# Gated cross-attention block: the first pass of head pair 0 is issued inside the last projection chunk, and the row-maximum matmul reads 2 rows

## The reference

```
x = x + tanh(g_xattn) * cross_attention(context, layernorm(x), mask)
x = x + tanh(g_ffn)   * ffn(layernorm(x))
cross_attention: k, v = split((context @ W_src.T + b_src) * mask);  q = (tgt @ W_tgt.T + b_tgt) * mask
                 8 heads of 64: softmax(q @ k.T / 8, keys with mask 0 at -inf) @ v, joined with tgt, @ W_out.T + b_out
ffn: 8-bit activations and ternary weights, 512 -> 2048, depthwise convolution of width 3, SiLU, 2048 -> 512
```

## Time and profile before

| | us |
|---|---|
| median of 3 runs | 1926.86 |
| the profiled execution | 1929.86 |
| its span, first to last instruction | 1928.0 |
| stages A and B up to the last matmul of chunk 7 | 610.69 |
| from there to the first score | 57.55 |
| first score to the end of the attention | 728 |

### The profile page before, as it was taken

How to read it: one execution, slowest core, us unless ns; L and a number is a source line. 1 busy time by engine, 2 the same in 40 slices (tenths; PEclk the granted TensorE clock), 3 DMA queues, 4 the chain that set the end, 5 groups by cost and what they waited for, 6 DMA issues and landing times.

```text
span 1928.0 us, 24398 instructions
## 1 busy us (share of the span) xinstructions
PE 1684.4 (87%) x8738; PEld 1038.8 (54%) x8738; DVE 1216.9 (63%) x2270; ACT 780.3 (40%) x793; POOL 729.0 (38%) x317
## 2 busy tenths in 40 slices
PE   6887899999997699999999999999856785967867
PEld 5666678888885344455445444544433443534434
DVE  6777645343433567755765676465269979799793
ACT  2111122222210044433442344245318766787676
POOL 1121000000000088866885688578606134062340
PEclk9989999999998599999999999999979798997988
DMA  6656547444444511114111412041130030120201
GB/s 233 229 181 206 179 170 243 154 149 152 171 145 152 180 56 56 56 66 143 56 57 66 143 57 100 12 143 35 44 131 1 1 131 0 38 92 0 88 1 44
DMA packets 104676, 200.59 MB, mean 104 GB/s; under 512 B 7568, under 2 KB 27024, under 8 KB 104592
## 3 DMA queue, kind: packets, MB, share of 16 engines
q1 hardware_dynamic: 104592, 199.49, 29.5%
HBM read 127.90 MB, written 71.57 MB: 103 GB/s over the span
## 4 chain that ended last, share of the span: by engine, by line
PE 62%; issue 19%; POOL 7%; DVE 6%; DMA 5%; SPq 1%; ACT 1%; POOLq 0%; DVEq 0%; ACTq 0%
PE ps L1260 13%; PE ps L1272 12%; PE ps L1224 9%; PE ps L1226 9%; PE ps L1225 9%; PE ps L1244 6%; DMA wraw<-in_w2T 5%; POOL h_first L672 4%; POOL h_third L672 2%; PE ps L1285 2%; DVE junk L926 1%; PE ps L1461 1%; DVE h_first L1179 1%; POOL acc L667 1%; DVE gp L1158 1%
## 5 line engine op out<-in xcount | busy, mean ns | idle before, releaser
L667 POOL TENSOR_TENSOR acc<-acc,pr 128x1024 f32<-128x1024 f32 x192 | 457.7, 2384 | 118.7 <-ACT pr L684 99.6
L684 ACT ACTIVATE pr<-ps,mcol 128x1024 f32<-128x1024 f32 x256 | 284.3, 1114 | 405.1 <-PE ps L1260 402.3
L926 DVE CUSTOM_DVE_ANT_0 junk<-ps,mbias 128x512 bf16<-128x512 f32 x512 | 333.4, 689 | 171.8 <-PE ps L1244 168.0
L1272 PE MATMUL ps<-pr,vv 128*64 128x512 f32 x1024 | 273.3, 616 | 0.0
L672 POOL TENSOR_TENSOR h_first<-h_first,last_tap 128x1024 f32<-128x1024 f32 x44 | 104.8, 2385 | 306.2 <-ACT last_tap L804 306.2
L650 POOL MEMSET nmt<- 128x128 f32 x1 | 0.2, 204 | 449.1 <-DMA w_ternary<-wtb 449.1
L1244 PE MATMUL ps<-kh,qh 64*128 64x512 f32 x512 | 136.8, 475 | 26.3 <-DVE nmv L926 17.6
L1244 PEld LDWEIGHTS ps<-kh,qh 64*128 64x128 f32 x512 | 57.5, 193 | 148.3 <-issue 101.7
L1419 PE MATMUL ps<-xiT,w1q 128*128 128x512 bf16 x512 | 125.1, 393 | 5.9 <-ACT xiT L790 5.9
L1461 PE MATMUL ps<-w2q,hq 128*128 128x512 bf16 x512 | 120.8, 390 | 2.5 <-ACT hq L840 1.8
L667 POOL TENSOR_TENSOR acc<-pr 128x1024 f32<-128x1024 f32 x32 | 76.8, 2399 | 110.8 <-ACT pr L684 110.8
(11 more groups left out here) (152 smaller groups left out, 3179.7 us busy)
## 6 DMA issues: line engine op xcount, KB each, us to landing
craw<-in_ctxT SPq DMA_DIRECT2D x8, 2048.0 KB, 9.7
xa<-in_x SPq DMA_DIRECT2D x8, 1024.0 KB, 6.4
wraw<-in_w1T SPq DMA_DIRECT2D x16, 512.0 KB, 7.3
wraw<-in_w2T SPq DMA_DIRECT2D x16, 512.0 KB, 7.6
q_split<-kqh SPq DMA_DIRECT2D x32, 256.0 KB, 2.0
q_split<-kql SPq DMA_DIRECT2D x32, 256.0 KB, 2.3
base<-lna SPq DMA_DIRECT2D x8, 1024.0 KB, 9.1
k_split<-kqh SPq DMA_DIRECT2D x32, 256.0 KB, 2.2
```

What stands on the lines that cost most here:

```text
L667: nc.gpsimd.tensor_tensor(acc[:, blk % 2, :], first, pr[:, (8 * blk + j) % NP, :], ALU.add).then_inc(pool_acc, 1)
L684: act.activation(pr[:, u % NP, :], ps[:, 2 * (u % 2):2 * (u % 2) + 2, :].rearrange("p a t -> p (a t)"), ACT.Exp, bias=mcol[:, (u // 64) * ...
L926: dve.tensor_tensor_reduce(out=junk[:, e, :], in0=ps[:, 4 + e, :], in1=mbias[:, b % 2, kk * CH:(kk + 1) * CH], scale=-1.0, scalar=3.0e38, ...
L1272: last = pe.matmul(ps[64 * e:64 * e + 64, 6 + blk % 2, :], vv[:, g % 2, j, 64 * e:64 * e + 64], pr[:, u % NP, e * CH:(e + 1) * CH], start= ...
```

## The change

The first 22 first-pass units are taken out of the front of stage C and put between the matmuls of chunk 7, on PE and on DVE. Up to unit 11 they use banks 4 to 7 in turn, from unit 12 to 21 banks 0 to 3, and a unit waits for the one two before it. `rows(0)` stands after the second value group. SP issues the loads of mask, `mcol`, `ql`, `kl` and `vv` before the stores of chunk 7, and stores and reads the row maxima between the stores of the values. ACT, not PE, now waits for the last stores of stage B, ahead of its first exponential.

```diff
@@ SP
             load_qk(0)
+            sp.wait_ge(pe_bv, (NCH - 1) * CT + 8)
+            load_mrow(0)
             load_qk(1)
+            sp.dma_start(mcol[:], mask_cols).then_inc(sp_mcol, 16)
+            load_lo(0)
...
+            load_vv(0)
             b_chunk(B - 1, 1, True)
@@ POOL
-            nc.gpsimd.memset(maug[:].bitcast(F32), 0.0).then_inc(pool_zero, 1)
@@ ACT, ahead of the first exp
+            act.wait_ge(dve_b, NCH * B_DVE_N)
...
+            act.wait_ge(sp_wq_out, 16 + 32 * NCH)
@@ order of the units
+        K_UNITS = {(m, part): 3 * m + part for m in range(PAIRS) for part in range(3)}
+        V_UNITS = {(0, 0): 12, (0, 1): 13, (0, 2): 14, (1, 0): 15, (2, 0): 16, (2, 1): 17, (2, 2): 18, (3, 0): 19, (3, 1): 20, (3, 2): 21}
@@ PE, unit n
+            if 2 <= n < LEAD:
+                pe.wait_ge(dve_free4, use4["t", 0] + 1 if n == 16 else use4["a", n - 2] + 1)
+                pe.wait_ge(dve_free5, use5["b", n - 2] + 1)
@@ PE, score
-                        last = pe.matmul(ps[:, 2 * (u % 2) + e, :], of_keys[64 * e:64 * e + 64, :], of_tokens[64 * e:64 * e + 64, :],
+                        part = slice(64 * e, 64 * e + (64 if w < 3 else 2))
+                        last = pe.matmul(ps[:, 2 * (u % 2) + e, :], of_keys[part, :], of_tokens[part, :],
                                          start=w == 0, stop=w == 3)
@@ PE, chunk 7
+                    def between(k):
+                        if k in (3, 6):
+                            pe_tops(pe, K_UNITS[m, k // 3 - 1])
+
+                    split_mm(pe, ps[:, m, :], ..., KS, between).then_inc(pe_bk, 1)
+                    pe_tops(pe, K_UNITS[m, 2])
@@ DVE, chunk 7
+                dve_bias(dve, 0)
+                dve.wait_ge(sp_mcol, 16)
...
+                for m in range(PAIRS):
+                    dve_tops(dve, K_UNITS[m, 0])
+                    dve_tops(dve, K_UNITS[m, 1])
+                    dve.wait_ge(pe_bk, (NCH - 1) * PAIRS + m + 1)
...
+                    dve_tops(dve, K_UNITS[m, 2])
```

More of the change, by code:

```diff
@@ L150, in flamingo_gated_block @@
         pr = sb("pr", [P, NP, 2 * CH], F32)
[L151 to L156, removed]
         un = sb("un", [P, 2, CH], F32)
-        aug1 = sb("aug1", [P, P], F32R)
-        nmv = sb("nmv", [P, 32], F32)
-        mcol = sb("mcol", [P, NCH * CT], F32)
         mt = sb("mt", [16, 2, P], F32R)
         zr = sb("zr", [P, 16], F32)
-        assert used["at"] <= CHL + SLOT
+        assert used["at"] <= TOP_AB
+        used["at"] = TOP_AB
+        vv, ql, kl, maug = [], [], [], []
+        for i in range(2):
+            vv.append(sb(f"vv{i}", [P, NT, P], F32))
+            ql.append(sb(f"ql{i}", [P, S], F32R))
+            kl.append(sb(f"kl{i}", [P, S], F32R))
+            maug.append(sb(f"maug{i}", [P, S], F32R))
+            if i == 0:
+                assert used["at"] == TOP_AB + SLOT
+                acc = sb("acc", [P, 2, 2 * CH], F32)
+        mbias = sb("mbias", [P, 2, S], F32)
+        assert used["at"] == CHL + SLOT
         used["at"] = CHL + SLOT
@@ L529, in b_chunk @@
                     sp.dma_start(vd[ds(c * CH + j * P, P), :], vst[:, j % 2, :]).then_inc(sp_v_out[j % 2], 16)
+                    if last and half and j == 1:
+                        max_out(0)
+                    if last and half and j == 2:
+                        max_rows(0)
                 sp.wait_ge(dve_b, c * B_DVE_N + B_DVE["wb1"])
@@ L694, in c_act @@
             act.wait_ge(dve_mbias, 2)
+            act.wait_ge(dve_b, NCH * B_DVE_N)
+            for sl in range(2):
+                act.wait_ge(sp_k_out[sl], 32 + 64 * NCH)
+            act.wait_ge(sp_wq_out, 16 + 32 * NCH)
             for s in range(MACROS):
@@ L913, in ln_steps @@
                     lambda: (maxes(4), scales()), lambda: integers(0), lambda: integers(4)]
-        def c_dve(dve):
[L916 to L946, removed]
@@ new lines, in dve_tops @@
+        def dve_tops(dve, n):
+            g, i, kk = n // 16, n % 16 // 2, n % 2
+            b = g // PAIRS
+            if n % 64 == 0 and b:
+                dve_bias(dve, b)
+            if n % 16 == 0 and g:
+                dve.wait_ge(dve_nm, g)
+            for e, free, use in heads(n):
+                dve.wait_ge(pe_mx, n + 1)
+                c = (8 * e + i) * 2 + kk
+                dve.tensor_tensor_reduce(out=(junk1 if n < LEAD and n % 2 else junk)[:, e, :], in0=ps[:, first_bank(n) + e, :], in1=mbias[:, b % 2, kk * CH:(kk + 1) * CH], scale=-1.0,
+                                         scalar=3.0e38, op0=ALU.add, op1=ALU.min, accum_out=nmv[:, c:c + 1]).then_inc(free, 1)
+            if n % 16 == 15:
+                dve.wait_ge(dve_free4, use4["a", n] + 1)
+                dve.wait_ge(dve_free5, use5["b", n] + 1)
+                if g:
+                    dve.wait_ge(pe_mt, g)
+                dve.tensor_reduce(nmt[:, 0:16], nmv[:].rearrange("p (c k) -> p c k", k=2), AX.X, ALU.min).then_inc(dve_nm, 1)
@@ L1234, in ln_row, with pe_tops, pe_rows @@
             last.then_inc(pe_row, 1)
-        def c_pe(pe):
[L1237 to L1246, removed]
+        def pe_tops(pe, n):
+            g, i, kk = n // 16, n % 16 // 2, n % 2
+            if n % 16 == 0:
+                pe.wait_ge(sp_qk[g % 3], 32 * (g // 3 + 1))
+            if n < 2:
+                pe.wait_ge(dve_b, (NCH - 2) * B_DVE_N + B_DVE[f"v{2 * n + 1}"])
+            elif n in (12, 13):
+                pe.wait_ge(dve_b, (NCH - 1) * B_DVE_N + B_DVE[f"k{2 * n - 23}"])
+            if 2 <= n < LEAD:
+                pe.wait_ge(dve_free4, use4["t", 0] + 1 if n == 16 else use4["a", n - 2] + 1)
+                pe.wait_ge(dve_free5, use5["b", n - 2] + 1)
+            for e, free, use in heads(n):
+                if n >= LEAD:
+                    pe.wait_ge(free, use)
+                last = pe.matmul(ps[:, first_bank(n) + e, :], qh[g % 3][64 * e:64 * e + 64, i * P:(i + 1) * P],
+                                 kh[g % 3][64 * e:64 * e + 64, kk * CH:(kk + 1) * CH], start=True, stop=True)
+            last.then_inc(pe_mx, 1)
+        def pe_rows(pe, g):
+            pe.wait_ge(dve_nm, g + 1)
+            pe.wait_ge(dve_free4, use4["t", g])
+            pe.transpose(ps[:, turn_bank(g), 0:P], nmt[:], ident[:]).then_inc(pe_mt, 1)
+        def c_pe(pe):
             def score(u):
@@ L1294, in c_pe @@
             pe.wait_ge(pool_split, POOL_ALL)
-            pe.wait_ge(dve_b, NCH * B_DVE_N)
-            pe.wait_ge(pool_zero, 4)
-            for n in range(16):
-                tops(n)
-            rows(0)
-            for n in range(16, LEAD):
-                tops(n)
+            pe.wait_ge(pool_zero, 3)
             for s in range(MACROS):
@@ L1391, in _, with last_chunk, between @@
                 b_chunk(0, half, half == 0)
-            with pe.Fori(1, B) as b:
+            with pe.Fori(1, B - 1) as b:
                 for half in range(2):
                     b_chunk(b, half, False)
-            pe.wait_ge(dve_b, (NCH - 1) * B_DVE_N + B_DVE[f"k{PAIRS - 1}"])
+            b_chunk(B - 1, 0, False)
+            def last_chunk():
+                c, half = NCH - 1, 1
+                pe.wait_ge(dve_cl, c * KS + KS)
+                for m in range(PAIRS):
+                    pe.wait_ge(dve_b, (c - 1) * B_DVE_N + B_DVE[f"k{m}"])
+                    def between(k):
+                        if k in (3, 6):
+                            pe_tops(pe, K_UNITS[m, k // 3 - 1])
+                    split_mm(pe, ps[:, m, :], lambda k: (wsh[:, k, m * P:(m + 1) * P], wsl[:, k, m * P:(m + 1) * P]),
+                             lambda k: (chh[:, half, k, :], chl[:, half, k, :]), KS, between).then_inc(pe_bk, 1)
+                    pe_tops(pe, K_UNITS[m, 2])
+                for j in range(CT):
+                    pe.wait_ge(dve_free4, use4["a", 10 + j // 2] + 1)
+                    pe.wait_ge(dve_free5, use5["b", 10 + j // 2] + 1)
+                    def between(k):
+                        if k in (3, 6) and (j, k // 3 - 1) in V_UNITS:
+                            pe_tops(pe, V_UNITS[j, k // 3 - 1])
+                    split_mm(pe, ps[:, 4 + j, :], lambda k: (chh[:, half, k, j * P:(j + 1) * P], chl[:, half, k, j * P:(j + 1) * P]),
+                             lambda k: (wsh[:, k, D:2 * D], wsl[:, k, D:2 * D]), KS, between).then_inc(pe_bv, 1)
+                    if j == 1:
+                        pe_rows(pe, 0)
+                    if (j, 2) in V_UNITS:
+                        pe_tops(pe, V_UNITS[j, 2])
+            last_chunk()
             c_pe(pe)
```

141 lines of the change are left out of this document (89 added, 52 removed).

## The result

The changed kernel takes 1977.4 us (median of 4 runs, 1976.27 to 1978.58), the kernel before beside it 1927.03 (1926.18 to 1930.02): a ratio of 1.0259, 95% interval 1.0241 to 1.0276, slower. 1971 was forecast, in a range of 1928 to 1990. The profiled executions took 1978.58 and 1929.86 us, 48.7 apart.

A forecast was written before the change was run, and what follows sets the result against it. PE was taken as the bound in the attention, while nobody works through between chunk 7 and the first score. 1929.86 - 29.6 + 73.7 = 1974.0 us profiled, median 3.0 lower: 1971 us; own range 1952 to 1984, stated range 1928 to 1990.

The forecast's parts named there:

- The stall at the start of the chunk: Chunk 7, first unit: PE waits for kh0 to land at 578.7, 9.6 us with nothing of the chunk issued.
- The low clock behind it: Chunk 7 after the stall: the clock falls, some 5 us of work at half speed cost 2.5 us more.
- units: Chunk 7 on PE: 22 first-pass units between projection matmuls, 0.62 us each, 13.6 us in all.
- `mcol`: Chunk 7: mask columns land about 583, PE needs unit 0's reduction at 586.7; no cost, but 4 us later would.
- After the chunk: Start of attention: ACT's second exponential ends 8.7 us after the last matmul, fifth score 3.8 later at 648.9; 29.6 us gained.
- the lower bound of 22: First part's smallest gain in us, if PE also waits for mcol and is slow again at the attention's start.
- The second part: Attention macros: 2 rows in place of 64 add three shape changes of 0.195 us in each of 126 macros, 73.7 us.
- 2 rows save nothing: Fourth product of a score: a slot takes 0.23 us with 128 rows or 64, so a gain is excluded.
- A free change: Rival, attention macros: no shape change between 32 and 64 rows, period 4.7, 1897 us; chance 0.17.
- a partial price: Rival, attention macros: only one half of each change's cost arises, 378 x 0.10 = 38 us, 1935 us; chance 0.09.
- The chunk at the low clock: Rival, chunk 7: waits for DVE keep the clock at 0.5, its 43.6 us take up to 87, about 1996 us; chance 0.04.
- the first part: Chunk 7 and attention start: 22 units moved into chunk 7 gain 29.6 us, bounds 22 to 35.

The follow-up runs named there:

- the seventh experiment: Changed kernel with 64 rows, loads for the units and mask moved earlier, chunk 7's ternary store behind its third value store: 1890.67 us, ratio 0.9802.
- the first experiment: Changed kernel with the fourth product reading 64 rows again, its two tiles filled with zeros by POOL: 1902.47 us, ratio 0.9871.
- early loads: Changed kernel with qh, kh of pairs 0 and 1 and mcol loaded during chunk 6's value groups, the mask ahead of its ternary store: 1968.21 us, ratio 1.021.
- reordered score: Changed kernel with the 2-row product put first in every even score, six shape changes a macro in place of seven: 1953.58 us, ratio 1.0135.

## Why the prediction was right

**The stall at the start of the chunk**: 9.16 us, forecast 9.6. **The low clock behind it**: 0.66 over 570 to 572, back at 1.00 from 581. PE worked at half speed from 577.38 to 580.9, which cost 1.7 us, forecast 2.5. Chunk, stall, clock and units together took 68.5 us from the first matmul (566.02) to the first score (634.55), before 43.6: 24.9 more, forecast 25.7. **`mcol`**: no cost, as forecast, but by 0.24 us and not by the 4 us of the text, and so partly by luck. The text let PE reach the third unit at half speed throughout, at 586.7; the clock rose earlier, and PE was there at 583.61. And it left out that DVE needs 1.3 us for the two reductions of the first unit once `mcol` is there.

**After the chunk** lies the one term that was mis-sized. ACT starts 5.2 us after the last matmul, as forecast, and its second exponential ends at 642.85. From there 3.8 us were forecast to the fifth score; it took 8.6. PE waited 3.21 us for ACT, the clock fell a second time (0.50 over 640 to 652), and what PE did from 641.90 to 651.46 went at half speed, the new slots too: that is 4.8 us. The text had this only as a reason for the lower bound of 22. So chunk and start together gave 26.0, not 29.6. With 64 rows the same wait is followed by a shorter low clock, and 28.7 come of the 29.6. With the wait for the ternary stores gone as well, in the seventh experiment, it stayed at 1.00.

**The second part**: forecast 73.7, measured 74.9 in the attention; by 126 x 3 changes 0.198 us each, taken 0.195. Its reason, that a change of tile rows costs like any other change of shape, is shown by 32 against 33 rows and by the order that saves one change (0.189). That 2 rows save nothing: the first experiment, with 64 rows again, is 75 us faster. POOL stayed off the path, 524.77 busy of 791.

**The rivals.** A free change is excluded (2010 us alone, not 1927), a partial price too: both halves, 0.10 in front and 0.10 behind, appear in every slot above. The chunk at the low clock did not occur: 54 us at 1.00.

The sum was 1974.0 for a profiled execution and 1978.58 came. Of the 4.6 missing, 3.6 are the first part, 1.2 the second and 0.9 the stage behind, less 1.05 for the earlier start. The medians are further apart, 1971 and 1977.4, since the profiled execution was taken as 3.0 us above the median and was 1.2.

## What to carry to other kernels

A smaller operand can be the dearer one: before a matmul reads fewer rows, look which tile of the array it then gets, count how often the shape changes in the loop, and take the price from a slot in the trace; here one zero row more, 33 in place of 32, was worth 73 us. Hoisting a pass into a busy stage paid here (26 us) even though its inputs came late; the earlier loads gave 9 us more. And each wait removed uncovers the next, so look also at what regular spacing gives the slow partner, before instructions are grouped for the sake of the fast one.

## What the runs showed of the hardware

- The step lies between 32 and 33 rows: 2005.8 and 1932.4 us. With 2 rows or with 32 the slots are alike (0.33 and 0.43).
- A change of shape costs about 0.10 us before and 0.10 behind it (512 streamed columns, granted clock 1.00); a lone 2-row product between 64-row ones costs both twice, 0.39 to 0.40 us.
- The granted clock has two levels in these traces, 1.00 and 0.50. At the start of the attention it stayed at 0.50 for different times once PE worked without a gap: 5 us in the kernel before, 3.4 with 33 rows, 3.6 with the first part alone; but 7.1 with 32 rows, and with 2 rows 8.1 (early loads), 8.6 (reordered score), 10.6 (after) and 16.4 us (2 rows in the kernel before). Behind the hole in chunk 7, where no 2-row product runs, it was 3.5 us in the kernel after and 5.9 in that with the reordered score. These are single profiles, and no experiment took the cause apart.
- In all four kernels in which PE waited 3.2 us for ACT at the start of the attention the clock came to 0.50, but not at one point: in the kernel after at about 638.9, 0.2 us after PE stopped, with the first part alone at about 644.4, when PE was busy again. Elsewhere it fell behind waits of PE of 2.15, 2.61 and 2.67 us and did not behind 2.44 and 2.52, so the length of the last wait alone does not tell it.
- One DMA issue on SP can itself take long: 12.90 us for `qh` of the third pair in the kernel with both starts cleared, directly behind three large loads, and 0.36 us for the same load in the kernel before, where those three were issued 34 us earlier.
